# A 16-channel mixing kernel: short-row bias tiles made by VectorE, bias matmuls two tiles behind instead of four, and store pieces issued by two engines

## What is computed

```python
rel = jnp.tril(idx[:, None] - idx[None, :]).astype(jnp.float32)
threshold = jnp.abs(L_multiplier * init_L)
pos = jnp.maximum(rel.max(axis=-1), threshold)[:, None]
nd = jnp.log(jnp.abs(c * rel) + 1.0) / (jnp.log(jnp.abs(c * pos) + 1.0) + EPS)
h = jax.nn.relu(nd[..., None] * W1[0] + b1)
bias = jnp.einsum('qkm,mh->qkh', h, W2) + b2
x = x + bias.transpose(2, 0, 1)[None]
...
wi = w + jnp.eye(m, dtype=w.dtype)
ret = jnp.einsum('BGMTS,GMN->BGNTS', x, wi)
hq = jnp.einsum('BGMTS,BTGIM->BGITS', x, qw1)
ret = ret + jnp.einsum('BGITS,BTGIM->BGMTS', hq, qw2)
hk = jnp.einsum('BGMTS,BSGIM->BGITS', x, kw1)
ret = ret + jnp.einsum('BGITS,BSGIM->BGMTS', hk, kw2)
ret = ret + jnp.einsum('BGMTS,BTGM->BGMTS', x, qdd)
ret = ret + jnp.einsum('BGMTS,BSGM->BGMTS', x, kdd)
```

## Time and profile before

| | us |
|---|---|
| median of 3 runs | 1018.52 (1011.3 to 1022.31) |
| the profiled execution's own time | 1017.06 |
| its span, first to last instruction | 1015.1 |
| TensorE matmul busy | 755.0 (74%) |
| ScalarE busy | 453.8 (45%) |
| VectorE busy | 373.5 (37%) |
| GpSimd busy | 344.3 (34%) |

### The profile page before, as it was taken

How to read it: one execution, slowest core, us unless ns; L and a number is a source line. 1 busy time by engine, 2 the same in 40 slices (tenths; PEclk the granted TensorE clock), 3 DMA queues, 4 the chain that set the end, 5 groups by cost and what they waited for, 6 DMA issues and landing times.

```text
span 1015.1 us, 37021 instructions
## 1 busy us (share of the span) xinstructions
PE 755.0 (74%) x17186; PEld 545.3 (54%) x17186; DVE 373.5 (37%) x358; ACT 453.8 (45%) x472; POOL 344.3 (34%) x189
## 2 busy tenths in 40 slices
PE   2269697688767796697965978777796687867973
PEld 1029654486536753485534955347553485534963
DVE  7970265205640274204541045310354103541041
ACT  6554264444553263443653435534264443653400
POOL 7461044202440053202863027630276402771000
PEclk9679988798979997789999989979899798996997
DMA  6974799844997178943899138892388923790079
GB/s 112 204 163 82 191 201 238 191 103 107 226 205 175 41 164 214 200 107 85 179 203 201 47 85 183 206 191 49 83 154 211 200 67 79 168 214 3 5 161 194
DMA packets 366437, 149.50 MB, mean 147 GB/s; under 512 B 99660, under 2 KB 366028, under 8 KB 366284
## 3 DMA queue, kind: packets, MB, share of 16 engines
q1 hardware_dynamic: 229068, 80.02, 39.3%
q10 hardware_dynamic: 137216, 67.13, 27.6%
HBM read 77.61 MB, written 69.47 MB: 145 GB/s over the span
## 4 chain that ended last, share of the span: by engine, by line
PE 42%; SPq 15%; ACTq 15%; ACT 9%; issue 8%; DMA 4%; POOL 3%; DVE 3%; POOLq 0%; DVEq 0%
PE main L609 22%; ACTq L196 15%; PE main L599 11%; PE bias L622 9%; SPq L223 9%; ACT hidden L376 4%; SPq L230 4%; POOL hidden L339 3%; ACT hidden L371 3%; DMA mats_a<-a_mats 3%; ACT y L385 2%; DVE mixed L510 1%; DMA a_mats<-mixed 1%; DMA b_mats<-mixed 1%; DVE y L523 1%
## 5 line engine op out<-in xcount | busy, mean ns | idle before, releaser
L339 POOL TENSOR_TENSOR hidden<-log_table,row_scale 128x1024 f32<-128x1024 f32 x176 | 340.1, 1950 | 573.4 <-PE bias L622 560.7
L376 ACT ACTIVATE hidden<-hidden,b_col 128x1024 f32<-128x1024 f32 x176 | 197.6, 1144 | 293.6 <-issue 153.5
L622 PE MATMUL bias<-hidden,w_blocks 128*64 128x512 f32 x768 | 229.9, 714 | 129.2 <-ACT hidden L376 84.3
L510 DVE TENSOR_TENSOR mixed<-main,mixed 128x1024 f32<-128x1024 f32 x128 | 156.7, 1224 | 440.0 <-PE main L599 440.0
L599 PEld LDWEIGHTS main<-y,mats_a 32*32 32x32 f32 x8192 | 241.9, 131 | 121.2 <-issue 58.4
L599 PE MATMUL main<-y,mats_a 32*32 32x128 f32 x8192 | 271.3, 280 | 42.1 <-DMA mats_a<-a_mats 28.0
L609 PE MATMUL main<-y,mats_b 32*32 32x128 f32 x8192 | 258.0, 281 | 51.1 <-issue 37.8
L609 PEld LDWEIGHTS main<-y,mats_b 32*32 32x32 f32 x8192 | 243.3, 132 | 74.4 <-issue 46.5
L398 ACT ACTIVATE mixed<-main 128x1024 f32<-128x1024 f32 x128 | 130.9, 1023 | 199.5 <-PE main L609 194.2
L622 PEld LDWEIGHTS bias<-hidden,w_blocks 128*64 128x64 f32 x768 | 54.8, 155 | 233.5 <-issue 189.3
L523 DVE SCALAR_TENSOR_TENSOR y<-bias,b_col,x_stage 128x1024 f32<-128x1024 f32 x64 | 82.2, 1284 | 142.7 <-PE bias L622 142.7
(11 more groups left out here) (37 smaller groups left out, 27.5 us busy)
## 6 DMA issues: line engine op xcount, KB each, us to landing
x_stage<-in_x SPq DMA_DIRECT2D x512, 128.0 KB, 5.3
out_mixed<-mixed ACTq DMA_DIRECT2D x256, 128.0 KB, 4.4
out_mixed<-mixed ACTq DMA_DIRECT2D x128, 256.0 KB
mats_a<-a_mats SPq DMA_DIRECT2D x256, 32.0 KB
b_mats<-mixed SPq DMA_DIRECT2D x2, 512.0 KB, 6.1
mats_b<-b_mats SPq DMA_DIRECT2D x8, 128.0 KB, 2.8
a_mats<-mixed SPq DMA_DIRECT2D x2, 512.0 KB, 9.5
mixed<-in_L_conv_kw SPq DMA_DIRECT2D x2, 128.0 KB, 2.6
```

Of the source, the lines that this page charges most:

```text
L339: nc.gpsimd.tensor_tensor(hidden_tile(h).rearrange("p (j s) -> p j s", j=ROWS), bass.AP(logs.tensor, logs.offset, [list(logs.ap[0]), [1, R ...
L376: nc.scalar.activation(hidden_tile(h), hidden_tile(h), ACT.Relu, bias=b1_col[:, 0:1])\
L510: dve.tensor_tensor(at, main[:, T % 2, :].rearrange("p (t s) -> p t s", t=ROWS), at, ALU.add).then_inc(main_taken, 1)
L622: mm = pe.matmul(bias[into, T % 2, at:at + BANK], w2_blocks[:, g, :], hidden_tile(hidden_index(k, T, g))[:, at:at + BANK], start=True, sto ...
```

## The change

LAG becomes 2. Every second hidden tile of group 1 (odd T) is made by VectorE, as the larger of scaled logarithm and -b1, and the rest of ReLU's result, b1 times W2, is added as a constant through a third column of `b2_col`; ScalarE's eight small operations are gone. Blocks 0 to 3 of each piece are stored by SyncE, blocks 4 to 7 by ScalarE, and ScalarE does ReLU ahead of the stores of a step, for tiles 0 and 1 right after the column phase. In setup the A matrices' compact form is made by GpSimd between its hidden tiles, the turned matrices are copied by ScalarE, and the last x chunks of region 0 are loaded before the B matrices.

```diff
-LAG = 4
+LAG = 2
...
-SPREAD = (2, 4, 4, 2, 2, 1)
+SPREAD = (2, 2, 2, 2, 2, 1)
...
-        b2_col = sb("b2_col", [P, 2])
+        b2_col = sb("b2_col", [P, 3])
+        neg_b1 = sb("neg_b1", [P, 1])
...
-        def row_by_row(k, T, g):
-
-            return groups_of(k) == 2 and g == 1 and T % 4 == 3
-
-        def nd_count(k, T, g):
-
-            return 1 + sum(not row_by_row(r, U, f) for r in range(k + 1) for U in range(TILES)
-                           for f in range(groups_of(r)) if (r, U, f) < (k, T, g))
+        def by_dve(k, T, g):
+
+            return groups_of(k) == 2 and g == 1 and T % 2 == 1
+
+        def made_through(k, T, g, on_dve):
+
+            return sum(by_dve(r, U, f) == on_dve for r in range(k + 1) for U in range(TILES)
+                       for f in range(groups_of(r)) if (r, U, f) <= (k, T, g))
...
             save_mats("b")
+            for q in range(XSLOTS, XCHUNKS):
+                load_x(q)
             sp.wait_ge(mats_out["b"], 2 * DMA)
             sp.wait_ge(mats_zeroed, 3)
             load_mats_b()
-            for q in range(XSLOTS, XCHUNKS):
-                load_x(q)
             save_mats("a")
...
+                    for i in range(PIECES):
+                        if T == piece_end(i):
+                            sp.wait_ge(main_taken, a_tile(k, T) + 1)
+                            for b in range(BLOCKS // 2):
+                                store_block(sp, k, i, b).then_inc(out_done[i], DMA)
...
-                sp.wait_ge(main_taken, a_tile(k, TILES - 1) + 1)
                 if k == HALF - 2:
-                    sp.wait_ge(nd_ready, nd_count(HALF - 1, TILES - 1, 0))
+                    sp.wait_ge(nd_ready, made_through(HALF - 1, TILES - 1, 0, False))
                     sp.dma_start(row_scale[:], late_scales).then_inc(scales_in, DMA)
...
+            def compact_part(i):
+
+                if i == 0:
+                    pool.wait_ge(weights_in["a"], 4 * DMA)
+                    rank_one(nc.gpsimd, "a", 0, comp["a"]).then_inc(pool_step, 1)
+                    steps[0] += 1
...
+                else:
+                    on = diagonal(comp["a"], BLOCKS)
+                    nc.gpsimd.tensor_tensor(on, on, diag["a"].rearrange("p (b m) -> p b m", b=BLOCKS), ALU.add)\
+                        .then_inc(comp_made["a"], 1)
...
+                    if k == 0 and T % 2 == 1 and T < 10:
+                        compact_part(T // 2)
...
-                    h = hidden_index(k, T, g)
-                    if row_by_row(k, T, g):
-                        act.wait_ge(hidden_used, h - RING + 1)
-                        act.wait_ge(scales_in, DMA)
-                        t0 = k * W + T * ROWS
-                        for j in range(ROWS):
-                            at = t0 - SLOTS * W * g + j
-                            one = nc.scalar.activation(hidden_tile(h)[:, j * W:(j + 1) * W], log_table[:, at:at + W],
-                                                       ACT.Relu, bias=b1_col[:, 0:1], scale=row_scale[:, (t0 + j) % PART:(t0 + j) % PART + 1])
-                        one.then_inc(hidden_ready, 1)
-                    else:
-                        act.wait_ge(nd_ready, nd_count(k, T, g))
+                    if not by_dve(k, T, g):
+                        h = hidden_index(k, T, g)
+                        act.wait_ge(nd_ready, made_through(k, T, g, False))
                         nc.scalar.activation(hidden_tile(h), hidden_tile(h), ACT.Relu, bias=b1_col[:, 0:1])\
                             .then_inc(hidden_ready, 1)
+
+            def take_turned(part):
+                for half in range(2):
+                    act.wait_ge(main_ready, half + (1 if part == "b" else 3))
+                    nc.scalar.activation(turned[part][:, half * COLS:(half + 1) * COLS], main[:, half, :], ACT.Copy)\
+                        .then_inc(main_taken, 1)
...
                     take_b(k, C)
                 for s in range(TILES + LAG):
+                    if k + 1 < REGIONS:
+
+                        U = s if s < 2 else s - LAG + 1
+                        if U < TILES and s != LAG:
+                            make_hidden(k + 1, U)
+                        U = s - LAG
+                        if groups_of(k + 1) == 1 and U >= 0 and U % XTILES == XTILES - 1:
+                            add_const_bias(k + 1, U)
                     for i, spread in enumerate(SPREAD):
                         part = s - piece_end(i) - 1
                         if 0 <= part < spread:
                             if part == 0:
                                 act.wait_ge(main_taken, a_tile(k, s - 1) + 1)
-                            for b in range(BLOCKS // spread * part, BLOCKS // spread * (part + 1)):
+                            share = (BLOCKS - 4) // spread
+                            for b in range(4 + share * part, 4 + share * (part + 1)):
                                 store_block(act, k, i, b).then_inc(out_done[i], DMA)
-                    if k + 1 < REGIONS:
-                        U = s - LAG + 1
-                        if 0 <= U < TILES:
-                            make_hidden(k + 1, U)
-                        U = s - LAG
-                        if groups_of(k + 1) == 1 and U >= 0 and U % XTILES == XTILES - 1:
-                            add_const_bias(k + 1, U)
...
+                    base = 2 if by_dve(k, T, 1) else 0
                     dve.scalar_tensor_tensor(out=y_rows(slice(0, P), row, ROWS), in0=falling(T % 2, 0, 0, P, ROWS),
-                                             scalar=b2_col[:, 0:1], in1=x_rows(slice(0, P), k, T, 0, ROWS),
+                                             scalar=b2_col[:, base:base + 1], in1=x_rows(slice(0, P), k, T, 0, ROWS),
...
+            def make_hidden(k, T):
+
+                h = hidden_index(k, T, 1)
+                dve.wait_ge(hidden_used, h - RING + 1)
+                dve.wait_ge(scales_in, DMA)
+                t0 = k * W + T * ROWS
+                for j in range(ROWS):
+                    at, of_row = t0 - SLOTS * W + j, (t0 + j) % PART
+                    one = dve.tensor_scalar(hidden_tile(h)[:, j * W:(j + 1) * W], log_table[:, at:at + W],
+                                            row_scale[:, of_row:of_row + 1], neg_b1[:, 0:1], ALU.mult, ALU.max)
+                one.then_inc(dve_hidden_ready, 1)
...
                         finish_tile(k, T)
                     if U is not None and k + 1 < REGIONS:
+                        if U + 1 < TILES and by_dve(k + 1, U + 1, 1):
+                            make_hidden(k + 1, U + 1)
                         add_bias(k + 1, U)
...
-                pe.wait_ge(hidden_ready, hidden_index(k, T, groups - 1) + 1)
+                pe.wait_ge(hidden_ready, made_through(k, T, groups - 1, False))
+                if by_dve(k, T, groups - 1):
+                    pe.wait_ge(dve_hidden_ready, made_through(k, T, 1, True))
...
-                if T == 6:
+                if T == 12:
```

117 lines of the change are left out of this document (65 added, 52 removed).

## The result

The changed kernel took 1068.06 us (median of 4 runs, 1059.61 to 1075.41), the kernel before 1018.69 beside it: a ratio of 1.0492, 95% interval 1.0375 to 1.0609. It is slower, as forecast, but by 49 us where 26 were forecast, and 0.06 us beyond the stated range of 960 to 1068. The profiled execution spans 1059.3 us, 44.2 more than the 1015.1 of before. It is one of the two short ones of its four (1061.44 and 1059.61, mean granted clock 0.88); the others took 1075.41 and 1074.68 at 0.86.

A forecast was written before the change was run, and what follows sets the result against it. Row phases were taken to bound the kernel, TensorE waiting for ScalarE first and GpSimd plus ReLU last, setting the pace between. Terms 0 - 6 + 31 + 6 - 5 = +26 us gave a 1044 us median, range 960 to 1068.

The forecast's parts named there:

- the turns: Two-group row phases: each GpSimd product falling into VectorE's eight small operations slips between two of them, costing 1.9 us.
- The walk: Step-by-step timeline of row phases: two-group pairs of steps 11.8 us against 8.75 before; one-group phases 69 us against 75.4.
- No turns: Rival, chance 0.22: small operations don't take both ports, or VectorE keeps them through all eight; about 948 us.
- The four two-group row phases: Row phases whose next region needs two groups of bias matmuls: mean 97.8 us against 90, +31 us for four.
- the clock stays up: Rival, chance 0.18: turns occur, but the clock stays high and SyncE hides; pairs of 10.8 us, 1005 to 1018 total.
- The column phases behind: Three column phases behind two-group row phases: more x loads issued inside them, +2 us each, +6 in all.
- the last region: End of the kernel: with stores issued from two queues only piece 5 follows the last add, -5 us.
- the split stores: Three one-group regions: -3 us for each of two row phases, nothing in the first; -6 us, bounds -35 and +15.
- setup: Before the first column phase: VectorE sheds the A products, GpSimd takes them; 0 us, bounds -3 and +6.
- SyncE is the bound in all regions: Rival, chance 0.10: SyncE's 120 issues a region need 1.1 us each, one-group regions lose 5 to 10; about 1070 us.

The follow-up runs named there:

- gpsimd_waits: Changed kernel with one added wait: GpSimd begins an even tile's products only when VectorE has made the tile before; 979.38 us, ratio 0.9704.
- fused: Changed kernel with one 128x1024 VectorE operation per hidden tile instead of eight, using only the first row's scale; 975.35 us, ratio 0.969.
- dve_only: Changed kernel with LAG 4, all stores on ScalarE and its order as before, VectorE's hidden tiles kept; 1073.76 us, ratio 1.066 to the kernel before.
- stores_on_act: Changed kernel with all eight DMAs of a store piece issued by ScalarE; 1053.32 us, ratio 1.0314 to the kernel before.
- half_x: Changed kernel with every second x chunk left out from the second region on (224 of 512 loads); 996.86 us, ratio 0.9811.
- a_once: Changed kernel with all loads of the A matrices after the first two chunks left out (240 of 256); 1023.34 us, ratio 1.0086.
- x_short: Changed kernel with all x loads issued, but each bringing 8 of 16 rows from the second region on; 1018.14 us, ratio 1.008.
- a_short: Changed kernel with all A loads issued, but each bringing half the matrix columns from the third chunk on; 1063.19 us, ratio 1.0457.
- no_dve: Changed kernel without VectorE's hidden tiles; ScalarE makes group 1 of every fourth tile again; 968.49 us, ratio 0.9608 to the kernel before.
- x_split: Changed kernel with GpSimd's added wait and SyncE's queue reordered, plus ScalarE issuing half the column phases' x loads from region 1; 971.25 us, 955.77 without that last edit.

## Why the prediction was right in sign and short in size

**The sign hung on the turns, and these held.** The walk had the eight operations at 1.7 us plus two products: 5.5 us for the eight, a tile 4.9 us after the bias tile before it, a wait of 2.9. Measured: 5.35 us, a wait of 2.86 in 28 of the 32 pairs, 95.6 us in all. That the sum of the eight came out is partly luck: alone they take 2.13 us, not 1.7, and the two products lengthen them by 3.2 us, not by their own 3.8; the two errors nearly cancel. The rival "No turns" priced a pair at 7.8 to 8.2 us and a phase at 73; where an experiment took the turns away a pair took 8.2 to 8.6 us (gpsimd_waits) and 7.9 to 8.2 (fused), and the two-group row phases 65 to 71. So its price for these phases was about right and its condition wrong; but the kernels took 975 to 979 us, not 948, as their column phases became longer (279 and 290 us for the six, 229 before). The turns cost 1.0492 - 0.9704 = 7.9% of 1018, 80 us, give or take 1.9% by the two intervals.

**The four two-group row phases**: +34.0 against +31. The pair was forecast at 11.8, with the clock falling in two of three; six pairs took 68.2 to 75.2 us, 11.4 to 12.5 each, and behind 23 of the 28 waits of 2.86 us the bias tile took more than its 1.94 us. In the seven kernels that have these pairs (changed, dve_only, stores_on_act, half_x, a_once, x_short, a_short) it was 129 of 186, two of three, just as forecast; the profile of the changed kernel had more falls than most. That "the clock stays up", the second rival, is refuted. The column phases behind, +8.2 against +6, and the last region, -4.1 against -5, both held.

**The term that failed is that of the split stores, -6 us for the one-group regions.** It had two halves. The row phases went as the walk said: "66 us", "69 against 75.4"; measured 70.5, 66.9, 67.2, with the A loads late at the thirteenth tile: "landed at 46", and at 46 us in the second of the three. What was missized is what stands behind: "Piece 5, behind eight A loads on SyncE, lands at 73, when the first copy of the column phase has wanted it for 3 us". It landed 78.6 us after the start of that row phase: SyncE's queue issued without a break from the x loads at 249.95 on, and ahead of the last eight A loads and of piece 5 stood eight more stores, 8.67 us of issues that the walk did not count. In three phases TensorE stood 16.8 us for ScalarE's first copies. And "half of that goes to x loads that start later" had no price for what these do to the column phase: the x loads begin 7 us behind its start, where before they began 11 us ahead (304.07 and 289.04; DMA share 0.74 against 0.60). The three column phases took 24.3 us more: 16.8 of it is that wait, 4.5 more gaps inside a tile (22.3 against 17.8), 3.1 more busy time at a lower clock. Sum: -21.9 and +24.3, +2.4 instead of -6. The other three profiles of the same program in these regions (no_dve, fused, gpsimd_waits) have +1.1, +7.9 and +17.1, so the miss is no accident of one profile, but its size is uncertain. With +2.2 in the first column phase, for which the forecast had no term, and +1.5 in setup, which it put at 0 within bounds of -3 and +6, that is 12 of the 18 us that the spans differ from the forecast; the other 6 are the +3, +2.2 and +0.9 of the terms above.

The rest, 5 us between spans and medians, is the spread between executions: the median of the changed kernel lies 6.6 us over its profiled one, that of before 1.6. It was not followed further.

**"SyncE is the bound in all regions"** was given 1060 to 1085, and the measured time lies in that band, but its mechanism is not what happened. In the two-group regions, which lost most, the waits are for VectorE, and x_split, with half of the column phases' x issues off SyncE, was no faster. (The 1.1 us an issue that the rival read from the A loads at 255 is 10.51 / 8 = 1.3.) It is true of the one-group *row phases* alone: 172 us with fewer issues, 205 with all.

The Trainium skill, "DMA: Bandwidth & Descriptors", section "Issuing engines are not separate DMA queues", says that a second issuing engine saves the sequencer's time and nothing else. No gain beyond it is seen: the last region gained 4.1 us, and over the whole kernel the split moved issues onto the busier queue (ratio 1.0492 against 1.0314).
